# A selective-scan kernel: GpSimd and ScalarE make the input term of two of every 16 scans

## The reference

```python
x = x + 0.5 * ffn(layernorm(x), w_gate, w_up, w_down)      # fp4 quantise/dequantise before each matmul
x = x + mixer(layernorm(x), ...)
x = x + 0.5 * ffn(layernorm(x), w_gate, w_up, w_down)
```

```python
xz = h @ in_proj_w;  x, z = split(xz);  x = silu(causal_conv4(x))
dt_r, Bm, Cm = split(x @ x_proj_w)                          # 64, 16, 16
delta = softplus(dt_r @ dt_proj_w + dt_proj_b)              # (1024, 512)
dA  = exp(delta[..., None] * A);  dBu = delta[..., None] * Bm[:, :, None, :] * x[..., None]
h_t = dA_t * h_(t-1) + dBu_t;     y_t = sum_n h_t[:, n] * Cm_t[n]
out = ((y + x * D) * silu(z)) @ out_proj_w
```

## Time and profile before

| | us |
|---|---|
| median of 3 runs | 3069.84 (3069.81 to 3070.99) |
| the profiled execution, its own time | 3067.41 |
| its span, first to last instruction | 3065.3 |
| the scans, start of the first to start of the last | 672.5 to 2495.7 |

### The profile page before, as it was taken

The page is one execution under the profiler, slowest core; times in us unless marked ns, Lnnn a source line. Parts: engine busy times, 40 slices in busy tenths (PEclk is TensorE's granted clock), DMA queues, the critical chain, the costliest instruction groups (busy, mean ns, idle before and its releaser), DMA issues. The chain is left out here.

```text
span 3065.3 us, 31487 instructions
## 1 busy us (share of the span) xinstructions
PE 2635.0 (86%) x10275; PEld 1370.1 (45%) x10275; DVE 2610.8 (85%) x2467; ACT 1718.6 (56%) x2305; POOL 2206.6 (72%) x1316
## 2 busy tenths in 40 slices
PE   5999999967878878878878878878877669999998
PEld 2666556633424424424424425425413126666665
DVE  7888865449999999999999999999999977777775
ACT  3555444456666666666666666666664534444442
POOL 4766654348888888888888888788788855655553
PEclk9999999979979979979979979979976679999999
DMA  3111111047787777787777777777776840111000
GB/s 111 31 52 52 42 48 35 28 116 181 169 196 179 186 193 177 179 197 174 187 191 173 187 194 171 191 188 176 188 176 168 209 111 24 35 35 31 30 28 21
DMA packets 173218, 387.95 MB, mean 127 GB/s; under 512 B 22544, under 2 KB 90064, under 8 KB 172816
## 3 DMA queue, kind: packets, MB, share of 16 engines
q1 hardware_dynamic: 154176, 365.49, 47.8%
q10 hardware_dynamic: 18896, 20.65, 2.3%
HBM read 308.33 MB, written 52.56 MB: 118 GB/s over the span
## 5 line engine op out<-in xcount | busy, mean ns | idle before, releaser
L1439 POOL TENSOR_TENSOR mix_scan<-mix_scan,mix_bc 128x1024 f32<-128x1024 f32 x512 | 1200.6, 2359 | 269.7 <-DVE mix_scan L1524 269.4
L1524 DVE TENSOR_TENSOR_SCAN mix_scan<-mix_decay,ps_all 128x1024 f32<-128x1024 f32 x512 | 1170.6, 2286 | 67.2 <-ACT mix_decay L1482 18.5
L878 PE MATMUL ps_all<-ffn_w_gate_up,ffn_xT 128*128 128x512 f32 (+1 forms) x1536 | 653.9, 562 | 14.2 <-DVE ffn_h L605 11.1
L1576 PE MATMUL ps_all<-mix_stack,mix_sel 96*128 96x512 bf16 x1024 | 359.2, 438 | 329.7 <-DVE mix_scan L1524 296.5
L1482 ACT ACTIVATE mix_decay<-mix_decay,mix_a_neg 128x1024 f32<-128x1024 f32 x512 | 574.2, 1142 | 120.6 <-DMA mix_decay<-delta_rows 119.8
L1535 DVE TENSOR_TENSOR ps_all<-ps_all,mix_bc 128x1024 f32<-128x1024 f32 x512 | 618.1, 1207 | 24.4 <-PE ps_all L1576 23.9
L878 PEld LDWEIGHTS ps_all<-ffn_w_gate_up,ffn_xT 128*128 128x128 f32 x1536 | 278.6, 192 | 246.0 <-issue 200.8
L1576 PEld LDWEIGHTS ps_all<-mix_stack,mix_sel 96*128 96x128 bf16 x1024 | 75.7, 102 | 652.5 <-DVE mix_scan L1524 538.4
L751 POOL TENSOR_TENSOR ffn_h_scaled<-ffn_h,ffn_h_recip 128x1408 f32<-128x1408 f32 x64 | 168.6, 2634 | 244.9 <-ACT ffn_h_recip L846 244.9
L605 DVE TENSOR_TENSOR ffn_h<-ffn_silu_gate,ps_all 128x704 f32<-128x704 f32 x128 | 113.7, 888 | 270.1 <-ACT ffn_silu_gate L793 266.2
L1558 PE MATMUL ps_all<-mix_scan,mix_red 128*32 128x512 f32 x2048 | 331.1, 727 | 7.0 <-POOL mix_scan L1439 4.8
(11 more groups left out here) (131 smaller groups left out, 3738.1 us busy)
## 6 DMA issues: line engine op xcount, KB each, us to landing
mix_decay<-delta_rows SPq DMA_DIRECT2D x512, 512.0 KB, 8.3
mix_stack<-mix_parts SPq DMA_DIRECT2D x384, 64.0 KB, 2.0
delta_rows<-mix_delta SPq DMA_DIRECT2D x32, 512.0 KB, 3.1
ffn_x<-_attn_hidden_states_dram SPq DMA_DIRECT2D x32, 256.0 KB, 2.9
after_ffn<-ffn_y SPq DMA_DIRECT2D x32, 256.0 KB, 3.0
normed_ffn<-ffn_y_normed SPq DMA_DIRECT2D x32, 256.0 KB, 3.2
mix_x_tokens<-normed_ffn SPq DMA_DIRECT2D x32, 256.0 KB, 12.6
mix_x_residual<-after_ffn ACTq DMA_DIRECT2D x32, 256.0 KB, 6.2
```

What stands on the lines that cost most here:

```text
L878: ins = M(psG[:, lo:hi], xT[:, j % 2, (t * KX + k) * P:(t * KX + k + 1) * P], wgu[:, k, lo:hi], start=(k == 0), stop=(k == KX - 1))
L1439: G.tensor_tensor(wt, wt, bc[r % 2][:, 1, :], ALU.mult).then_inc(hc_done, 1)
L1524: V.tensor_tensor_scan(w[:, slot % RING, :], da[:, slot % SPREADS, :], ps_du[:, slot % 2, :], 0.0, ALU.mult, ALU.add).then_inc(scan_done, 1)
L1576: ins = M(ps_du[:, slot % 2, h * 512:(h + 1) * 512], const.sel[0:SEL, i, :], stack[:, c % 2, q, h * 512:(h + 1) * 512], start=True, stop=True)
```

## The change

Slots 7 and 15 of every chunk (64 of the 512) get their dBu another way. TensorE makes no delta*u for them and VectorE makes no product with B. Instead:

- SyncE stores 24 rows of delta*u of each chunk to DRAM (`keep_du`, 96 KB), in slot 6 ahead of the restack there, and `leave1`, which overwrites delta*u in place, waits for that store (`du_kept`).
- SyncE spreads 8 of these rows over the 128 partitions of a new tile `aside` (`spread_du`, 512 KB written), seven slots ahead, which is slots 0 and 8 of a chunk, ahead of the spread of delta of that slot.
- GpSimd multiplies `aside` by B in place, four slots ahead, which is slots 3 and 11, after its product with C of that slot.
- ScalarE copies the product into `ps_du`, one slot ahead, at the very head of its slots 6 and 14. It waits for GpSimd and for the scan that last read that buffer.
- The scan waits for this copy.

The small selection matrix `sel_bc` now shares its place with `w_dt`, and two waits are added where the constants are made.

```diff
+        dt_sel = a.sb("w_dt_and_sel_bc", [P, DI])
+        self.w_dt = dt_sel[0:RANK, :]
+        self.sel_bc = dt_sel[:, 0:2 * P].rearrange("p (w n) -> p w n", w=2)
...
+            sp.wait_ge(self.const_step, 1)
             for to, of in loads:
...
+            if j == 5:
+                pool.wait_ge(self.mixer_loaded, self.mixer_loads)
...
+EVERY, ASIDE_IN, ASIDE = 8, 7, 4
+ASIDE_FROM = 104
...
+    def keep_du(sy, b, par, c):
+        sy.wait_ge(du_done, chunk(b, c))
+        sy.dma_start(du_dram[par, c, :, :], du[ASIDE_FROM:P, :]).then_inc(du_kept, 16)
...
     def leave1(pool, n):
         pool.wait_ge(cast1, n)
+        pool.wait_ge(du_kept, 16 * n)
...
+            def spread_du(r, R, slot):
+                c, s = divmod(slot, SLOTS)
+                if s == EVERY - 1:
+                    sy.wait_ge(du_kept, 16 * chunk(R, c))
+                if slot >= EVERY or r > 0:
+                    sy.wait_ge(aside_put, nth_aside(R, slot) - 1)
+                row = 32 * (s % 4) + 8 * (s // 4) - ASIDE_FROM
+                sy.dma_start(aside[:, :],
+                             du_dram[r % 2, c, row:row + NCH, :].unsqueeze(0).to_broadcast([NST, NCH, L]))\
+                  .then_inc(aside_in, 16)
...  (SyncE)
+                        if s - LATER[c] == CAST1:
+                            keep_du(sy, b, rb % 2, cc)
...
+                    rr, R2, at = ahead(r, R, slot, ASIDE_IN)
+                    if core(rr, full) and is_aside(at):
+                        spread_du(rr, R2, at)
...  (GpSimd)
+                    rr, R2, at = ahead(r, R, slot, ASIDE)
+                    if core(rr, full) and is_aside(at):
+                        pool.wait_ge(aside_in, 16 * nth_aside(R2, at))
+                        G.tensor_tensor(aside[:, :], aside[:, :], bc[rr % 2][:, 0, :], ALU.mult)\
+                         .then_inc(aside_done, 1)
...  (ScalarE)
+                    if core(r, full) and is_aside(slot + 1):
+                        act.wait_ge(aside_done, nth_aside(R, slot + 1))
+                        act.wait_ge(scan_done, R * 64 + slot)
+                        A.activation(ps_du[:, (slot + 1) % 2, :], aside[:, :], ACT.Copy).then_inc(aside_put, 1)
...  (VectorE)
-                dve.wait_ge(dbu_done, n)
+                if is_aside(slot):
+                    dve.wait_ge(aside_put, nth_aside(R, slot))
+                else:
+                    dve.wait_ge(dbu_done, nth_vector(R, slot))
...
-                    if core(r, full):
-                        n = R * 64 + (slot + 1)
-                        dve.wait_ge(rep_du, n)
+                    if core(r, full) and not is_aside(slot):
+                        dve.wait_ge(rep_du, nth_vector(R, slot))
...  (TensorE)
-                    if slot < 63 and core(r, full):
+                    if slot < 63 and core(r, full) and not is_aside(slot + 1):
                         replicate(r, R, slot + 1)
```

More of the change, by code:

```diff
@@ L89, in __init__ @@
         self.w_x = a.sb("w_x", [P, CHUNKS, XP])
-        self.w_dt = a.sb("w_dt", [RANK, DI])
+        dt_sel = a.sb("w_dt_and_sel_bc", [P, DI])
+        self.w_dt = dt_sel[0:RANK, :]
+        self.sel_bc = dt_sel[:, 0:2 * P].rearrange("p (w n) -> p w n", w=2)
         self.w_out = a.sb("w_out", [P, CHUNKS, D])
@@ L103, in __init__ @@
         self.sel = a.sb("sel", [P, 4, P], BF16)
-        self.sel_bc = a.sb("sel_bc", [P, 2, P])
         self.red = a.sb("red", [P, 4, 4, NCH])
@@ L1055, in mixer @@
     xres = a.sb("x_residual", [P, 4, 2, D])
+    aside = a.sb("dbu_aside", [P, L])
     ps_job = [bank(psum, 0), bank(psum, 7)]
@@ L1059, in mixer @@
     delta_dram = nc.dram_tensor("delta_rows", [2, DI, L], F32, kind="Internal").ap()
+    du_dram = nc.dram_tensor("delta_u_rows", [2, CHUNKS, P - ASIDE_FROM, L], F32, kind="Internal").ap()
     S = a.sem
+    du_kept, aside_in, aside_done, aside_put = S("du_kept"), S("aside_in"), S("aside_dbu_done"), S("aside_put")
     x_in = [S("x_in0"), S("x_in1")]
@@ L1102, in job_list, with is_aside, nth_aside, nth_vector @@
                 for m, (s, k, rel, n) in enumerate(mine)]
+    def is_aside(slot):
+        return slot % EVERY == EVERY - 1
+    def nth_aside(R, slot):
+        return R * (64 // EVERY) + (slot + 1) // EVERY
+    def nth_vector(R, slot):
+        return R * (64 - 64 // EVERY) + (slot + 1) - (slot + 1) // EVERY
     def nth(kind, b, n):
@@ L1312, in first_sync @@
             keep_delta(sy, 0, 0, 0)
+            keep_du(sy, 0, 0, 0)
         if k in (43, 44):
```

## The result

| | before | after |
|---|---|---|
| median of the runs, taken in turn (15 each) | 3069.49 | 3075.04 |
| the profiled execution's span | 3065.3 | 3072.9 |
| start of the first scan to end of the last | 672.5 to 2498.0 | 670.2 to 2503.5 |

The ratio is 1.0019, 95% interval 1.0011 to 1.0027: the changed kernel is slower by 0.19%, a little and surely. The forecast had the opposite sign. All of the difference is in the mixer, 7.7 us of the two profiled executions.

The account below looks back on a forecast made before the run. VectorE was taken to bound the scans, with GpSimd's lag eating most of the 83 us spared: six middle rounds -1, first and last -2 each, in all -5 us, giving 3065 (own range 3058 to 3076; with neighbours 3032 to 3096).

Parts of the forecast that it names:

- What bounds the kernel, and that GpSimd's lag decides and not its rate: Scan stage: VectorE bounds it at 96% busy; GpSimd's added products fit its rate, but its lag is the bound.
- GpSimd's chain: From slot 3, seven more operations run without a gap until slot 13; the new product moves them 2.31 us later.
- Chunk 0, +1.9: Slot 15: ScalarE's table load and silu stand ahead of the new copy, so scan 15 is late; cost 1.9 us.
- Chunk 1, -0.3: Late restack and slot 15's spread leave 0.3 of 2.6 us saved; slot 11's 0.8 is contained in that stop.
- Chunk 2, +0.4: First saved product brings nothing, second 1.3 us, against silu and the new spread; cost 0.4 us (-0.8 to +1.5).
- Chunk 3, -2.1: Later chain and GpSimd's idle time hide all but 0.4 us of the new product; gain 2.1 us.
- The first and last rounds, -2 each: First round: chunk 0 has no gate; last: no silu, chunk 0 gains 1.5 us; -2 us taken for each.
- The new transfers at 0, at most 2.24 a chunk: Spreads for slots 7 and 15 have time in the queue: 0 taken, at most 2.24 us in chunks 0 to 2.
- The port, 3%: Rival, 3%: GpSimd's 64 new products stop VectorE for their length through the shared SBUF port, adding 148 us: 3135.
- All kept, 5%: Rival, 5%: everything VectorE is spared, 83 us, is kept, giving 2987; needs GpSimd's 2.31 us to vanish.
- The sum: Middle round -0.1 us, six of them -1, first and last rounds -2 each; in all -5 us, 3065.
- The signs: VectorE's idle before scans grows some 75 us, GpSimd's wait falls to about 120; wrong if waits stand at other slots.

Follow-up runs that it names:

- e1: Changed kernel (slots 7 and 15 aside), but GpSimd's product with B covers 16 of 1024 columns: 3035.0 us, ratio 0.9888.
- e4: Changed kernel, but only slot 15 of every chunk is made aside, its product in slot 11: 3035.4 us, ratio 0.9885 to the kernel before.
- e19: Only slot 15 aside, chunk 0's quarter of silu in slot 14 in place of 13: 3022.2 us, ratio 0.9857 to the kernel before.
- e2: Changed kernel, but the aside transfer moves only 8 rows to 8 partitions (32 KB, not 512 KB): 3064.1 us, ratio 0.9984.
- e3: Changed kernel with both the 16-column GpSimd product and the 32 KB transfer: 3022.2 us, ratio 0.9848 to the kernel before.
- e5: Changed kernel, but only slot 7 of every chunk is made aside, its product in slot 3: 3087.7 us, ratio 1.0071 to the kernel before.
- e18: As e14, but TensorE's output job of chunk 1 in round slot 28 instead of 27: 3067.9 us, ratio 1.0008 to the kernel before.
- e14: Changed kernel with second and third casts one slot later and chunk 1's z jobs one slot earlier: 3043.5 us, ratio 0.9915.
- e6: Only slot 15 aside, quarters of silu of chunks 0 and 2 in round slots 14 and 46: 3025.9 us, ratio 0.9861.

## Why the prediction was wrong, point by point

- *What bounds the kernel, and that GpSimd's lag decides and not its rate*: right. GpSimd's products cost 40 us (e1) although it was idle for 151.6 us before others.
- *GpSimd's chain*: the prediction counts seven more operations for the next chunk and the gate; the rows have five (L1150, L1184, L1155, L1165, L1173). None of its times hangs on the count.
- *Chunk 0, +1.9*: right, by its mechanism. Scan 15 waited 2.91 for a copy behind table load and silu, and taking silu out of the way gave 1.5, of which 1.2 at scan 15 (e4 against e19). That it is right to the tenth is partly luck: 0.6 of it is a stop at scan 4, of 1.1 in the three of six rounds in which TensorE's clock was low there.
- *Chunk 1, -0.3*: this is the step that failed; +1.3 was measured. The prediction followed the late `leave1` to slot 11 (0.8; 0.7 measured) and to the restack and slot 15, and said that the 0.8 were contained in that later stop. It left out one consumer of the same cast: silu(z), behind it on ScalarE, then the output job and `replicate`. In the sum this was a term put at nothing without a word; it measured 3.0 a round, of which some 0.6 is the lower clock in two of the rounds. That stop of 2.3 to 4.0 is larger than the one at slot 15 and comes ahead of it, so that it swallows it: slot 15 then gives its full 1.2. Seen from the sum, the step should have read -1.3 + 0.7 + 3.0 - 1.2.
- *Chunk 2, +0.4*: -0.2, near it with two things cancelling that it doesn't have. The first product saved brought nothing, as said: at full clock scans 7 and 8 together are 1.7 over their beat before and after. But in four of six rounds the clock fell there and they are 3.4 over (in round 3 scan 7 waited 2.42 us for its copy, and the next product 2.07 for TensorE, where it had waited 1.59), 1.1 a round; and at scans 4 and 5, where the clock was low in five of six rounds before and in one after, 1.1 a round came back. The second product saved brought 0.3. *Chunk 3, -2.1*: -1.6.
- *The first and last rounds, -2 each*: -1.5, and +1.0. In the last chunk of all the spreads landed late (that of `aside` for slot 7 took 17.9 us), and scan 6 waited 5.44 us for its exponential; its interval is 4.3 longer than before the change. The prediction took only the gates and silu of this round into account, not its transfers:

```profile
2471.38 2.29 DVE L1584 TENSOR_TENSOR_SCAN mix_scan<-mix_decay,ps_all 128x1024 f32<-128x1024 f32 x1 [5.44 <-ACT mix_decay L1539]
```

- *The new transfers at 0, at most 2.24 a chunk*: too low, inside the bound. They cost 11 us (e2), and the one in front of the spread for slot 14 of chunk 1 made the restack behind it slower too: a 64 KB DMA took 4.9 (median 2.0; 2.0 to 2.6 in e2 at this place), and the spread for slot 15 6.4 where it took 4.8 (4.9 in e2). The DMA view of after at 1462.9:

```profile
mix_decay<-delta_rows SPq DMA_DIRECT2D x1, 512.0 KB, 6.4
mix_stack<-mix_parts SPq DMA_DIRECT2D x1, 64.0 KB, 4.9
```

- *The port, 3%*: rightly low. GpSimd's product with C has a mean of 2364 ns after and 2359 before, the scan 2285 and 2286, with 64 more GpSimd products beside VectorE. The Trainium skill ("Perfetto Trace Analysis", Optimizing Scalar/DVE Operations) warns of a port shared by the two; these rows show no sign of it for operations with one operand in PSUM. The prediction gives one condition of the Trainium skill's page "SBUF — State Buffer" (Who interferes with whom), two inputs in SBUF; the section has a second one, VectorE's modes that use two ports, on which no run here bears. *All kept, 5%*: e3 shows that even with products and transfers all but free only 47 of the 83 us are kept.
- *The sum*: a middle round -0.1, measured +1.4. Over six rounds that is 9 us, nearly all from chunk 1 (1.6 a round), and 3 more came in the last round.
- *The signs*: one of those named for being wrong came true, waits at another slot (13). VectorE's idle time before scans grew by 60 us and not 75, and 21 more came before products; GpSimd's wait for scans fell to 151.6 and not 120.
- *TensorE's clock*: the prediction has no term for it, nor had any expectation. It decides 1 to 2 us a round in several places, and it both gave and took.

What is shown: that slot 7 carries the loss (e4, e5), that GpSimd's product is its main part (e1), that the output job is the last link at slot 13 (e18). That the wait of ScalarE's second cast is what makes it late in after is shown by the rows and by e14, where the job is on time in the one middle round in which the clock held. Not shown is what sets the clock.

The version that beats both is e19: only slot 15 aside and silu of chunk 0 one slot later, 3022.2 against 3064.6 of before, ratio 0.9857 (0.9838 to 0.9876). e6 is within that interval.

## What to carry to other kernels

Work moved to an engine that runs without a gap costs nothing at once: it delays each thing behind it, so list every consumer of each delayed step, down each engine's order, and not only the first two that you find; the stop that comes first and is largest is the one that counts. Put such work right before a gap of that engine (slot 15's product gained 34 us), not at the head of its longest chain (slot 7's lost 21). And an operation that changes ScalarE's table brings two loads, so see what stands behind the second. And before a stop that is there in some rounds and not in others is put down to an order of operations, compare the granted clock of the two.
